# The last attention's sums split over two parts of its output product, the places of the experts' rows worked out ahead of the gates' values, and the later quads' chains moved between tiles

## What is computed

```
# L3 attention (a gated running state, 8 heads of 64)
q, k, v = x @ Wq + bq, x @ Wk + bk, x @ Wv + bv
attn    = softmax over heads of (q . k) * scale
state   = decay * state + (1 - decay) * attn * v         # scan over the tokens
aug     = sigmoid(q * aug_param)
out     = (q * state + aug) @ Wo + bo                    # then a layernorm with scale and bias
# L3 second mixer: x += sigmoid(layernorm(x)) * wkv, with wkv of the context alone
# L3 feed-forward: 14 experts, two of them for each token
probs   = softmax(layernorm(x) @ gate_w.T)
w, idx  = top 2 of probs, w normalised to sum 1
out     = sum of the two w * (gelu(h @ w1[idx] + b1) @ w2[idx] + b2)
x       = x + clip(h + out, -100, 100)                   # h = layernorm(x)
```

## Time and profile before

| what | us |
|---|---|
| median of 3 runs | 1617.22 (1616.95 to 1620.99) |
| profiled execution | 1602.95 |
| its span | 1600.8 |
| TensorE busy (matmul) | 1366.5 (85%) |
| VectorE busy | 1181.1 (74%) |
| ScalarE busy | 872.2 (54%) |
| GpSimd busy | 777.0 (49%) |
| mean granted clock of TensorE | 0.936 |

### The profile page before, as it was taken

The page is one execution under the profiler, slowest core; times in us unless marked ns, Lnnn a source line. Parts: engine busy times, 40 slices in busy tenths (PEclk is TensorE's granted clock), DMA queues, the critical chain, the costliest instruction groups (busy, mean ns, idle before and its releaser), DMA issues. The chain is left out here.

```text
span 1600.8 us, 28454 instructions
## 1 busy us (share of the span) xinstructions
PE 1366.5 (85%) x9686; PEld 896.0 (56%) x9694; DVE 1181.1 (74%) x2532; ACT 872.2 (54%) x2666; POOL 777.0 (49%) x743
## 2 busy tenths in 40 slices
PE   5999787899789999898898987999996788837774
PEld 2665455555567775563343433788884444427774
DVE  5888577789677775465888898777777679885535
ACT  3775333377577772216767764777774343424532
POOL 4557453222555441414898887333354133553433
PEclk9999998999899999999999999999998898858887
DMA  7000000000000000001000000000004000023444
GB/s 309 1 2 1 1 2 1 1 2 2 1 2 2 2 2 0 1 13 83 1 1 0 1 1 1 1 2 2 2 2 138 0 1 1 1 71 99 142 142 142
DMA packets 42526, 47.06 MB, mean 29 GB/s; under 512 B 2576, under 2 KB 35984, under 8 KB 41616
## 3 DMA queue, kind: packets, MB, share of 16 engines
q1 hardware_dynamic: 40336, 41.05, 7.7%
q0 software_dynamic: 2048, 4.20, 0.9%
HBM read 31.08 MB, written 14.16 MB: 28 GB/s over the span
## 5 line engine op out<-in xcount | busy, mean ns | idle before, releaser
L837 POOL TENSOR_TENSOR l_xattn_probs<-l_xattn_probs,l_xattn_recip 128x512 f32<-128x512 f32 x128 | 133.3, 1041 | 220.0 <-DVE l_xattn_recip L776 219.6
L1034 ACT ACTIVATE l_attn_probs<-ps,l_attn_neg_max 128x128 f32<-128x128 f32 x512 | 145.4, 386 | 71.5 <-DVE l_attn_neg_max L1096 69.8
L2752 POOL TENSOR_TENSOR l_mamba_hc<-l_mamba_h,l_mamba_c 128x512 f32<-128x512 f32 x128 | 159.2, 1271 | 0.0
L2673 DVE TENSOR_TENSOR_SCAN l_mamba_h<-ps,l_mamba_dBx 128x512 f32<-128x512 f32 x128 | 152.5, 1210 | 1.8 <-ACT ps L2570 0.7
L2446 PE MATMUL ps<-l_mamba_hc,w_const 128*128 128x512 f32 x256 | 136.3, 638 | 19.3 <-POOL l_mamba_hc L2752 16.5
L771 DVE COPY l_xattn_probsT<-ps 128x512 f32<-128x512 f32 x128 | 87.9, 687 | 69.7 <-PE ps L623 69.7
L246 POOL TENSOR_TENSOR rs<-rs,neg_half 128x4 f32<-128x4 f32 (+2 forms) x32 | 43.5, 1358 | 152.8 <-DVE rs L240 152.7
L722 ACT ACTIVATE l_xattn_probs<-ps,l_xattn_neg_max 128x128 f32<-128x128 f32 x256 | 91.8, 388 | 41.3 <-DVE l_xattn_neg_max L766 41.3
L722 ACT ACTIVATE l_xattn_probs<-l_xattn_biased,l_xattn_neg_max 128x128 f32<-128x128 f32 x256 | 99.4, 392 | 12.2 <-DVE l_xattn_neg_max L766 12.2
L2570 ACT ACTIVATE ps<-l_mamba_th,l_mamba_w_a_bias,l_mamba_w_a_scale 128x508 f32<-128x508 f32 x128 | 97.1, 782 | 13.4 <-DVE l_mamba_h L2673 12.7
L1096 DVE TENSOR_REDUCE l_attn_neg_max<-ps 128x8 f32<-128x1024 f32 x64 | 78.1, 1221 | 26.7 <-PE ps L924 26.7
(11 more groups left out here) (578 smaller groups left out, 3645.4 us busy)
## 6 DMA issues: line engine op xcount, KB each, us to landing
w_l_xattn<-in_l_moe SPq DMA_DIRECT2D x28, 257.0 KB, 4.1
sorted_in<-l_nothing SPq DMA_DIRECT2D x4, 1344.0 KB, 11.6
sorted_out<-l_wide SPq DMA_DIRECT2D x8, 512.0 KB, 3.9
w_early<-in_l_moe SPq DMA_DIRECT2D x1, 3688.0 KB, 12.1
l_large<-sorted_in SPq DMA_DIRECT2D x4, 576.0 KB, 6.5
w_l_xattn<-in_l_xattn SPq DMA_DIRECT2D x1, 2176.0 KB, 18.6
l_large<-sorted_in SPq DMA_DIRECT2D x4, 512.0 KB, 4.4
w_early<-in_l_xattn SPq DMA_DIRECT2D x1, 1890.0 KB, 11.6
```

The source lines that it names most:

```text
L837: nc.gpsimd.tensor_tensor(probs[:, D % 2, n, :, :], probs[:, D % 2, n, :, :], along(recip[:, D % 2, n, :], [P, HALF, P]), ALU.mult).then_i ...
L1034: ins = nc.scalar.activation(probs[:, t % 4, g, :], S_of(t)[:, g * P:(g + 1) * P], ACT.Exp, bias=neg_max[:, t % 2, g:g + 1], accum_out=total)
L2673: nc.vector.tensor_tensor_scan(flat(h[:, t % 2, half, :, :]), G.ps[:, DA_BANK[half], :], flat(dBx[:, t % 2, half, :, :]), 0.0, ALU.mult, A ...
L2752: nc.gpsimd.tensor_tensor(heads4(hc[:, t % 4, half, :]), h[:, t % 2, half, :, :], c_sb[:, t % 3, :, :], ALU.mult).then_inc((hc0_set, hc1_s ...
```

## The change

It has three parts.

1. **The last attention.** For quad 3 GpSimd's `add_aug` is gone. TensorE multiplies `aug` with Wo in `project_aug`, behind `rank(0)`, with the bias, into the bank that is kept open; `project_last` adds the product of the states, and stands ahead of the first `turn_rows`. The first products follow the first `turn_rows`, and the second `turn_rows` follows them. SyncE's wait for the sums of all chunks becomes one for states and `aug`.
2. **Places ahead of gates.** `best_two` ends with `which`; the gates' values are a function of their own, `gates_of`, which runs behind `place`. For quad 0 both stand ahead of `received_spreads(1)`, and GpSimd's `received_scales(1)` stands between the halves of the scatters.
3. **The later quads' chains.** `attended_spreads(2)` goes into the scans of quad 3, `receptance(2)` and `receive(2)`, `received_spreads(2)` and `place(1)` go ahead of the tile loop, and the steps of quads 1 to 3 stand at other n. The combines of quads 0 and 1 move from n = 36 and 41 to 28 and 37.

The diff:

```diff
--- before.py
+++ after.py
@@ -2922,7 +2922,8 @@
                 if q == 0:
                     sp.wait_ge(s_made, NQ)
                 if q == 1:
-                    sp.wait_ge(o_set, CH * NQ)
+                    sp.wait_ge(prod_set, CH * NQ)
+                    sp.wait_ge(aug_set, CH * NQ)
                 for lo, hi in LOADS:
                     if q == 0 and hi == TILES:
                         sp.wait_ge(prod_set, CH * LAST + 2)
@@ -3035,6 +3036,24 @@
                                           w["wo"][:, c * D:(c + 1) * D], start=False, stop=c == CH - 1, skip_group_check=True)
                 if j == QUAD - 1:
                     mm.then_inc(out_made, 1)
+
+            def project_aug():
+                pe.wait_ge(p_copied, NQ)
+                pe.wait_ge(aug_set, CH * NQ)
+                nc.tensor.matmul(G.ps[:, O_BANK[LAST], :], G.c["ones_row"], w["bo"].unsqueeze(1).broadcast_to([1, QUAD, D]), start=True,
+                                 stop=False, skip_group_check=True)
+                for j in range(QUAD):
+                    for c in range(CH):
+                        nc.tensor.matmul(G.ps[:, O_BANK[LAST], j * P:(j + 1) * P], aug[:, c, j * P:(j + 1) * P],
+                                         w["wo"][:, c * D:(c + 1) * D], start=False, stop=False, skip_group_check=True)
+
+            def project_last():
+                pe.wait_ge(prod_set, CH * NQ)
+                for j in range(QUAD):
+                    for c in range(CH):
+                        mm = nc.tensor.matmul(G.ps[:, O_BANK[LAST], j * P:(j + 1) * P], state_of(LAST, c)[:, j * P:(j + 1) * P],
+                                              w["wo"][:, c * D:(c + 1) * D], start=False, stop=c == CH - 1, skip_group_check=True)
+                mm.then_inc(out_made, 1)
 
             def turn_attended(q):
                 pe.wait_ge(t_normed0, 2 * (q + 1))
@@ -3108,6 +3127,7 @@
                                      start=True, stop=True).then_inc(p_made, 1)
                     if (q, c) == (LAST, 1):
                         rank(0)
+                        project_aug()
                     if (q, c) == (LAST, 2):
                         turn_tokens(1)
                     if c >= 2 and q + 2 < NQ:
@@ -3221,28 +3241,29 @@
                 attend(q)
             rate(1)
             add_biases(0)
+            project_last()
             turn_rows(0)
-            turn_rows(1)
             first(0)
             first(1)
-            for j in range(QUAD):
-                project(LAST, j)
+            turn_rows(1)
             for n in range(PAIRS * NQ):
                 second(n)
-                if n + 3 in begun_at:
+                if n == 0:
+                    rank(1)
+                if n > 0 and n + 3 in begun_at:
                     turn_rows(begun_at[n + 3])
                 if n + 2 < PAIRS * NQ:
                     first(n + 2)
-                if n in (0, 13, 25):
-                    rank(1 + n // 12)
-                if n in (3, 16, 27):
-                    turn_gates(1 + n // 12)
-                if n in (8, 19):
-                    turn_tokens(2 + n // 19)
-                if n in (9, 20):
-                    rate(2 + n // 20)
-                if n in (12, 24, 30):
-                    add_biases({12: 1, 24: 2, 30: 3}[n])
+                if n in (3, 13, 24):
+                    turn_gates(1 + n // 11)
+                if n in (5, 16):
+                    turn_tokens(2 + n // 16)
+                if n in (6, 17):
+                    rate(2 + n // 17)
+                if n in (9, 20, 27):
+                    add_biases({9: 1, 20: 2, 27: 3}[n])
+                if n in (10, 21):
+                    rank(2 + n // 21)
 
         @block.scalar
         def _(act):
@@ -3373,19 +3394,18 @@
                 attend(q)
             act.wait_ge(G.loaded["l3_moe"], 16)
             exponentials(1)
+            receptance(LAST - 1)
+            take_out(LAST)
             for n in range(PAIRS * NQ):
                 gelu(n)
-                if n == 1:
-                    take_out(LAST)
-                    receptance(LAST - 1)
-                if n in (4, 17, 28):
+                if n in (4, 14, 25):
                     take_gates(1 + n // 12)
-                if n == 14:
+                if n in (6, 17):
+                    take_tokens(2 + n // 17)
+                if n in (8, 19):
+                    exponentials(2 + n // 19)
+                if n == 12:
                     receptance(LAST)
-                if n in (9, 20):
-                    take_tokens(2 + n // 20)
-                if n in (11, 22):
-                    exponentials(2 + n // 20)
 
         @block.vector
         def _(dve):
@@ -3562,6 +3582,9 @@
                 for k in range(2):
                     link.note(nc.vector.scalar_tensor_tensor(which[:, k, :, :], count, float(k + 1), gates[:], ALU.is_equal, ALU.mult))
                 link.catch()
+
+            def gates_of(q):
+                wide = along(total[:], [P, QUAD, E])
                 link(nc.vector.tensor_tensor(gates[:], gates[:], scores[:], ALU.mult))
                 link(nc.vector.tensor_tensor(total[:], top8[:, :, 0], top8[:, :, 1], ALU.add))
                 link(nc.vector.tensor_scalar(total[:], total[:], 1e-10, None, ALU.max))
@@ -3691,8 +3714,9 @@
                     round_x(f + 1)
                 if q == LAST:
                     best_two(0)
+                    place(0)
+                    gates_of(0)
                     received_spreads(1)
-                    place(0)
                 if f == LAST:
                     add_down(f)
                 scan(q, 0)
@@ -3705,6 +3729,8 @@
                     add_down(f)
                 if f + 1 < NQ:
                     times_gate(f + 1, 0)
+                if q == LAST:
+                    attended_spreads(2)
                 scan(q, 2)
                 if f < LAST:
                     normals(f)
@@ -3719,53 +3745,57 @@
                     times_gate(f + 1, 3)
                 if 0 < q < LAST:
                     apply(q - 1)
-            attended_spreads(2)
+            receive(2)
             copy_rows(0)
+            best_two(1)
             copy_rows(1)
-            best_two(1)
+            received_spreads(2)
+            place(1)
             for n in range(PAIRS * NQ):
-                if n + 3 in begun_at:
+                if n > 0 and n + 3 in begun_at:
                     copy_rows(begun_at[n + 3])
                 if n == 1:
-                    place(1)
+                    gates_of(1)
                     weights_of(1)
+                if n == 2:
+                    received_here(2)
                     take_biases(0)
-                if n == 2:
+                if n == 3:
                     stats(LAST)
-                if n == 3:
-                    receive(2)
-                    received_spreads(2)
                 if n == 6:
                     apply(LAST)
                 if n == 7:
-                    received_here(2)
+                    below_max(2)
+                if n == 8:
+                    best_two(2)
                 if n == 10:
-                    below_max(2)
+                    attended_spreads(3)
                 if n == 11:
-                    attended_spreads(3)
+                    place(2)
+                    gates_of(2)
+                    weights_of(2)
                 if n == 12:
-                    best_two(2)
-                if n == 14:
-                    place(2)
-                    weights_of(2)
                     take_biases(1)
-                if n == 15:
+                if n == 13:
                     receive(3)
                     received_spreads(3)
+                if n == 16:
+                    received_here(3)
                 if n == 18:
-                    received_here(3)
-                if n == 21:
                     below_max(3)
+                if n == 19:
+                    best_two(3)
+                if n == 22:
+                    place(3)
+                    gates_of(3)
+                    weights_of(3)
                 if n == 23:
-                    best_two(3)
-                if n == 26:
-                    place(3)
-                    weights_of(3)
                     take_biases(2)
-                if n == 36:
+                if n == 28:
+                    combine(0)
+                if n == 32:
                     take_biases(3)
-                    combine(0)
-                if n == 41:
+                if n == 37:
                     combine(1)
                 if n in ended_at:
                     copy_y(ended_at[n])
@@ -3879,26 +3909,28 @@
                 if q == LAST:
                     apply_here(q - 1)
                     add_out(q - 1)
+                    scatter(0, 0)
                     received_scales(1)
-                    scatter(0, 0)
                     scatter(0, 1)
                 if f + 1 < NQ:
                     scale_x_up(f + 1)
                 if f == LAST:
```

(12 more changed lines are left out.)

## The result

| what | before | changed |
|---|---|---|
| median of 7 runs | 1617.22 us (1612.77 to 1620.99) | 1608.98 us (1604.46 to 1611.02) |
| profiled execution, span | 1602.95, 1600.8 | 1608.98, 1607.0 |
| ratio of the times | | 0.9943, 95% interval 0.9921 to 0.9965 |

The change gains 8.2 us, 0.6%. The forecast of 1588.2 and its range up to 1601 were both too fast. That turned out to be the key.

What follows compares the result with a forecast made beforehand. TensorE's waits for quads' rows from HBM, 26 us in the last 200, were taken as the bound. 27.2 us at the last products plus 1.6 at the end, say 29, gave 1617.2 - 29 = 1588.2 us; range 1581 to 1601.

Steps and rivals of the forecast that it cites:

- First tile: Last attention to the experts' second product: that product at about 1441.7 instead of 1448.26, 6.5 us earlier, bounds 5 and 8.
- Quad 1: Start of quad 1 on TensorE: 1466.4 instead of 1474.75, 8.4 us earlier, bounds 6 and 10, a 3 us gap left.
- Quads 2 and 3, the last products: Tile loop: quad 2 12.8 us earlier without a gap, quad 3 22.7 earlier, last products 27.2 earlier.
- The stall of gelu behind receptance: Quad 2, pair 12: gelu queues behind receptance, which waits for GpSimd's shift; costed at 2 to 3.5 us.
- the Trainium skill's 1.38: ScalarE table switches: a drain of about 1.38 us each would grow gelu's stall by 2.8 us, whole gain about 26.
- the part on the end: After the last products: earlier combines of the first quads save 1.6 us; store, eight gathers and last combine stay.
- The base: Sums made against the profiled execution of 1602.95 us, then put on the median of 1617.22, 14.3 above it.
- VectorE did not take the place of the rows: Rival, quads 2 and 3: VectorE work ahead of the tile loop keeps 3 us gaps; gain 15, 1602; chance 0.18.
- The scatters did not get slower: Rival, scatters beside VectorE's densest chains take 0.5 us more each, a gap reopens; gain 23; chance 0.07.
- The lock of the shared port: Skill rule behind the slower-scatters rival: VectorE and GpSimd share an exclusive port lock; locked-out GpSimd can't write descriptors; chance 0.07.
- the pattern of short waits: Rival, tile loop: scattered short waits drop TensorE to 1.2 GHz, 84 us more at worst, 1672; chance 0.03.

Runs made afterwards that it cites:

- quiet trace: Changed kernel, unchanged, traced once more: 1568.52 us, 159.9 us from the probabilities to the end.
- stalling trace: First trace of the changed kernel, against the kernel before: 1608.98 us, 196.6 us from the probabilities to the end.
- quiet set: Runs on one chip without common stalls; changed kernel against the kernel before in one: 1580.45 us against 1603.75, ratio 0.9844.
- stalling trace of the kernel before: Kernel before, unchanged, run again on a chip with common stalls: 201.9 us from the probabilities to the end.
- spaced gathers: Changed kernel with a 0.9 us memset behind each gather of quads 0 to 2: 1579.22 us first, 1585.72 us (ratio 0.9801) the second time.
- half of the gathers: Changed kernel with four gathers in place of eight for quads 0 to 2: 1575.49 us first; last products at 158.8 us the second time.

## Why the prediction was wrong, point by point

Counted from the probabilities (forecast: its times less 1409.34; measured: the quiet trace less its 1406.62, and the first trace of the changed kernel less its 1410.43):

| step | before | forecast | quiet trace | stalling trace |
|---|---|---|---|---|
| second product | 38.9 | 32.4 | 35.0 | 35.0 |
| quad 1 | 65.4 | 57.1 | 58.9 | 59.3 |
| quad 2 | 104.1 | 91.3 | 89.7 | 94.4 |
| quad 3 | 140.8 | 118.1 | 115.6 | 145.8 |
| last products | 169.1 | 142.0 | 139.1 | 175.7 |
| end | 191.5 | 162.7 | 159.9 | 196.6 |

- **First tile.** 3.9 us earlier, not 6.5, below the bound of 5. The scans were 1.22 us each, as forecast, but the last state came at 25.0 us, not 23.9. The second part of the projection took 6.2 us, from 1431.63 to 1437.81 in the quiet trace, not 5.3: the granted clock was 0.57 there. From its end to the second product it took 3.8 us, not 3.2.
- **Quad 1.** 6.5 us earlier where 8.4 was forecast, just within the bounds of 6 and 10; the mechanism is right, with a gap of 2.7 us where 3 was forecast.
- **Quads 2 and 3, the last products.** In a quiet set right, with their mechanism: waits for rows of 1.1 and 0 us, and 14.4, 25.2 and 30.0 us gained, where 12.8, 22.7 and 27.2 were forecast. The stall of gelu behind receptance was 3.5 us, at the upper end of 2 to 3.5. ScalarE's rows there show the table load of 1.28 at 1476.99 and the gelu at 1478.28, with no drain behind it, so the Trainium skill's 1.38 (ScalarE: Activation LUTs, What ACT_TABLE_LOAD costs) isn't seen here either.
- **The step that failed** is in the part on the end: "the store, the eight gathers and the last combine stay", and of the gathers before them only that nothing waited for them. The gathers of quads 0 to 2 and the dense scatters were priced at nothing beside the tile loop, as work of another queue. Where the chip stalls, they cost 31 to 37 us there, against 10 when most of them lay in the waits for rows; that leaves 5 to 7 of the 28 to 32 us that the change saves in a quiet set. I asked of VectorE's work what covers it, not of GpSimd's transfers, whose cover were the very gaps that the change removed.
- **The base.** The sum was made against an execution of the quiet kind and taken off a median of the other. The 14.3 us between the two were noted as a fact to carry along. They were the sign that the timed runs held something that the trace didn't show: the common stalls, some 10 us, and a late start of the stage. In the stalling trace of the kernel before the probabilities begin at 1415.05, in the first at 1409.34; that this was early is luck.
- **The rivals.** None was it. VectorE did not take the place of the rows. The scatters did not get slower (most of the 32 took 0.96 us in every trace looked at; the longest took 1.8 where it had been 1.44, alike in the quiet and the stalling ones). The lock of the shared port is not the cause either. By the Trainium skill (SBUF — State Buffer, Who interferes with whom) the engine that issues second is blocked until the other's instruction is done, and ScalarE never waits on another. Here VectorE's copy is 9.1 us late, while seven separate DMA instructions of GpSimd with 0.30 us between them go by, and ScalarE is late as well. The clock did fall to 0.50, but behind the stalls, not by the pattern of short waits that I had named.

**What stays open.** What the indirect DMAs and the compute engines contend for, and what makes a chip or a set one of the stalling kind; each set was another chip, so the two can't be told apart. One trace sign goes with it: stalling traces lack many completion events. The changed kernel's quiet traces hold 2310 and 2312 events of DMA completion, its stalling ones 1335, 1335 and 1360. Over all twenty traces it is 1312 to 1562 in the stalling ones, the spaced gathers' second one among them, and 2310 to 2320 in the quiet ones (2116 with half of the gathers). The list of DMA issues shows it as a missing last column, the median time to landing; quiet, then stalling:

```profile
l_large<-sorted_in SPq DMA_DIRECT2D x4, 576.0 KB, 6.6
ctx<-sorted_out,l_places POOLq DMA_INDIRECT x16, 4.5
```

```profile
l_large<-sorted_in SPq DMA_DIRECT2D x4, 576.0 KB
ctx<-sorted_out,l_places POOLq DMA_INDIRECT x16
```

So the contended thing may be the path of semaphore events, or the path on which they are recorded. That VectorE and ScalarE start late with their input ready fits either. Each timed run was recorded as well, so the runs can't tell the two apart, and an execution that isn't recorded might not stall. This is the largest open point: if it is the recording, the 31 to 37 us are a cost of measuring, and the 28 to 32 us of the quiet sets are what the change is worth.

## What to carry to other kernels

Waits of the compute engines are also cover for other queues: before removing one, list every transfer that ran under it, the indirect ones above all, and price it beside a busy loop. Leave room between indirect DMAs that stand many in a row beside such a loop; 1 us behind each was worth some 20 us on a chip that stalls and cost nothing that could be told on one that doesn't. When engines seem to wait for one another, look up when the input of each late instruction was done: here that showed two engines late by themselves. And a profile that is faster than all timed runs by more than their spread is of another condition: take it again before building a sum on it.

## What the runs showed of the hardware

- Two conditions, constant within each set that was run, that differ by 10 us for one kernel and by 31 to 37 for another: three of the sets here, and the first comparison with its 14 runs, were of the stalling kind, two of the quiet one. The first trace of the kernel before is of the quiet kind; it is none of those 14 runs.
- A common stall: beside eight or more indirect DMAs in a row that start every 1.25 us, VectorE and ScalarE have waits of 5 to 17 us without a recorded release and start 4 to 16 us after their input is done; TensorE waits for them, and GpSimd keeps its pace.
- Upstream of the change the same instruction began anywhere between 1403.9 and 1421.5 us in twenty traces. Against this spread a change in one stage is best read from a mark inside the traces.
